# Moving ScalarE's Square pass over the mask from layer 0's slots to layer 1's

## The reference, cut to what matters

```python
x = layernorm(x + L0(x, adj))   # softmax over rows of leaky_relu(s1 + s2), masked by adj == 0
x = layernorm(x + L1(x, adj))   # masked by adj > 0, softmax over columns, then elu
x = layernorm(x + L2(x, adj))   # masked by adj > 0, softmax over rows, with a bias, then elu
x = layernorm(x + L3(x, adj))   # relation layer: one mask (adj == r) for each r of 1 to 4
```

## Time and profile before

| what | value |
|---|---|
| time of the kernel, median of 3 runs | 443.77 us |
| lowest and highest of the runs | 443.39 and 444.32 us |
| span of the profiled execution, first to last instruction | 440.8 us |
| the profiled execution's own time | not listed apart; the runs' times stand some 3 us above its span |
| busy, share of the span: PE, PEld, DVE, ACT, POOL | 83%, 74%, 84%, 72%, 67% |
| Square passes (L703) | 16, from 29.3 to 121.3 us, 1999 ns each |
| mean granted clock of TensorE | 0.952 |

### The profile page before, as it was taken

One profiled execution on the slowest core, in us unless ns is written; L12 is line 12 of the kernel. 1 busy time (PEld: TensorE's weight loads), 2 busy tenths in 40 slices (PEclk: granted clock), 3 DMA queues, 4 the chain that ended last, 5 costly groups with the idle time before them and its releaser, 6 DMA issues. The chain is left out here.

```text
span 440.8 us, 9222 instructions
## 1 busy us (share of the span) xinstructions
PE 366.6 (83%) x2770; PEld 326.6 (74%) x2777; DVE 368.5 (84%) x1406; ACT 316.0 (72%) x814; POOL 294.1 (67%) x430
## 2 busy tenths in 40 slices
PE   2689999999977776976787799899999789898860
PEld 1689999999877776876787799889888674454540
DVE  0067999999999999999999988889898987887862
ACT  2378999999855865655755867778787667877853
POOL 3226889977656644545463676888788867788782
PEclk9999999999988989898898999999999999999995
DMA  6999664000000000000000000000000000012122
GB/s 159 220 248 250 142 127 78 0 2 1 3 1 2 0 1 1 1 1 2 1 1 1 1 1 2 0 2 2 0 1 4 0 1 1 25 72 74 67 77 75
DMA packets 8756, 18.19 MB, mean 41 GB/s; under 512 B 1280, under 2 KB 2560, under 8 KB 8704
## 3 DMA queue, kind: packets, MB, share of 16 engines
q0 software_dynamic: 2304, 8.39, 10.0%
q1 hardware_dynamic: 5280, 8.72, 5.6%
q10 hardware_dynamic: 1120, 0.46, 0.5%
HBM read 21.76 MB, written 4.19 MB: 59 GB/s over the span
## 5 line engine op out<-in xcount | busy, mean ns | idle before, releaser
L486 PE MATMUL o_ps<-h_scaled,PT 128*128 128x129 f32 (+1 forms) x1536 | 190.3, 285 | 2.5 <-DVE PT L911 1.2
L486 PEld LDWEIGHTS o_ps<-h_scaled,PT 128*128 128x128 f32 x1536 | 186.2, 202 | 3.5 <-issue 1.7
L690 ACT ACTIVATE X<-y,offset,rstd 128x128 f32<-128x128 f32 x256 | 105.0, 481 | 47.9 <-POOL offset L277 47.9
L911 DVE SCALAR_TENSOR_TENSOR PT<-rows_ps,factors,MT 128x512 f32<-128x512 f32 x128 | 88.8, 737 | 0.6 <-PE rows_ps L473 0.2
L434 PE MATMUL h_ps<-wx,xT 128*128 128x130 f32 x384 | 58.8, 301 | 24.8 <-DVE smax L866 24.1
L434 PEld LDWEIGHTS h_ps<-wx,xT 128*128 128x128 f32 x384 | 52.5, 208 | 31.7 <-issue 31.5
L268 POOL TENSOR_TENSOR rstd<-var_eps,neg_half 128x4 f32<-128x4 f32 x64 | 68.9, 1077 | 5.0
L983 DVE BATCH_NORM_STATS2 stats<-y 128x6 f32<-128x128 f32 x256 | 56.0, 281 | 6.7 <-DVE y L963 0.5
L283 POOL TENSOR_TENSOR elu_exp<-elu_exp,X 128x512 f32<-128x512 f32 x32 | 40.8, 1274 | 15.0 <-ACT elu_exp L684 14.7
L258 POOL TENSOR_TENSOR h_scaled<-hx,factors 128x516 f32<-128x516 f32 x32 | 33.7, 1052 | 19.9 <-ACT factors L650 10.2
L906 DVE SCALAR_TENSOR_TENSOR PT<-MT,empty_col,edge 128x512 f32<-128x512 bf16 x64 | 44.3, 744 | 0.0
(11 more groups left out here) (104 smaller groups left out, 596.0 us busy)
## 6 DMA issues: line engine op xcount, KB each, us to landing
MT<-adj_by_j POOLq DMA_DIRECT2D x16, 512.0 KB, 8.8
X<-x SPq DMA_DIRECT2D x16, 256.0 KB, 6.5
out<-X SPq DMA_DIRECT2D x16, 256.0 KB, 2.0
w_rel<-w SPq DMA_DIRECT2D x1, 256.0 KB, 5.1
w_back<-w_by_output ACTq DMA_DIRECT2D x1, 192.0 KB, 3.3
wx<-w_by_input ACTq DMA_DIRECT2D x1, 192.0 KB, 5.5
bias<-b ACTq DMA_DIRECT2D x1, 64.0 KB, 4.6
bias<-b SPq DMA_DIRECT2D x1, 64.0 KB, 5.8
```

The costliest lines, as they stand in the source:

```text
L486: last = pe.matmul(o_ps[it.b][:, ic, first:1 + D], PT[:, it.b, jc, ic * P:(ic + 1) * P], h_scaled[:, it.b, jc, first:1 + D], start=(jc == ...
L690: last = act.activation(X[:, g, c, :], y[:, b, c, :], ACT.Identity, bias=offset[:, b, c:c + 1], scale=rstd[:, b, c:c + 1])
L911: dve.scalar_tensor_tensor(out=PT[:, it.b, c, :], in0=rows_ps[:], scalar=factors[:, it.b, 1, c:c + 1], in1=m, op0=ALU.max, op1=ALU.mult, * ...
```

## The change

The pass is called for `at(0)` at the end of ACT's `attention_slot`. The condition on the layer is the only thing that changes:

```diff
@@ -742,7 +742,7 @@
                 if n == -1:
                     act.wait_ge(sem("b2_ps"), 1)
                     act.copy(b2_a[:, :], o_ps[1][:, 0, 0:2]).then_inc(sem("b2_a"), 1)
-                if at(0) and at(0).l == 0:
+                if at(0) and at(0).l == 1:
                     flag(at(0))
 
             def relation_slot(at, n):
```

## The result

The changed kernel takes 465.65 us (median of 4 runs, 464.71 to 467.43), the kernel before, measured beside it, 443.58 (442.67 to 444.32). The ratio is 1.0502, with a 95% interval of 1.046 to 1.0544: slower by 22 us, near the forecast of 466.5 us and inside its range. The profiled execution is the run of 464.71 us; its span is 462.7, 21.9 us longer than before. The ratios in this document leave out two slow executions, one of 916.30 us in the first experiment and one of 452.32 us in the third, and no run shows what happened in them.

The account below looks back on a forecast made before the run. Bound: PE at 5.94 us a slot in layer 0, DVE at 8.28 in layer 1, where the change makes the ACT-POOL ring bind; -0.7 + 1.99 + 20.4 + 1.0 = +22.7 on span 440.8, plus 3.0: 466.5 us, range 456 to 472.

Parts of the forecast that it names:

- Layer 0, a gain of 0.7: Layer 0 loses 16 Squares; 13 slots go from 6.00 to 5.94 us each, gaining 0.7 us.
- The floor: Layer 0: PE still needs 5.94 us a slot without ACT's load.
- The upper bound of 5.1: Layer 0: the most to gain, 5.1 us, if only DVE's busy time of 5.61 us a slot were the limit.
- Slots 16 and 17, hidden: First two slots of layer 1: ACT's 4.03 us wait for PE's rows covers the passes, cost 0.
- Slot 18, +1.99: Layer 1, slot 18: the Square is exposed on ACT, so slot 19's take_rows starts 1.99 us later.
- The collision: Layer 1: late neg_mean and offset on POOL fall under DVE's line 906 and end only at its next 0.67 us step.
- Slots 19 to 30 at 9.88 us, +20.4: Layer 1: the closed ACT and POOL chain bounds 12 slots at 9.88 us, plus 2.15 for bias copies; 20.4 us lost.
- Slot 31, +1.0: Last slot of layer 1: 0 to 1.99 us of the pass shows, taken as 1.0.
- The rest gives nothing back: Everything else costs 0, and layer 2 and what follows pass ACT's lateness through whole.
- Rival A: Layer 1: POOL is not delayed by line 906, slots of 9.10 us, total +13.3, 457.1 us; chance 0.17.
- Rival B: Layer 1: POOL's rstd falls under line 906 too, 8.0 us more, 474.5 us; chance 0.13.
- Rival C: Layer 1: the pass hides within DVE's 8.28 us slot, 443.1 us, or 438.7 at the lower end; chance 0.07.

Follow-up runs that it names:

- the first experiment: The changed kernel with the same layer 1 passes moved ahead of the normalization in ACT's queue: 444.48 us, ratio 1.0008.
- the third: The kernel before, with POOL finding rstd and offset of the item before ahead of elu_low: 449.11 us, ratio 1.0102.

## Why the prediction was right, point by point

**Layer 0, a gain of 0.7.** Slots 0 to 13 took 77.66 us against 77.95, a gain of 0.29. The floor was right: most slots took 5.95 us. But two of 6.10 and 6.15 us (32.23 to 38.33, 62.19 to 68.34) came up though layer 0 has no pass any more, so the assumption that every slot would be at the floor failed here. In the experiment without a pass it held, with a gain of 0.72. Either gain is below what a run can tell. The upper bound of 5.1 is excluded by the experiment without a pass.

**Slots 16 and 17, hidden.** Right. ACT still waits for PE's rows before slot 18's take_rows; the cover was 4.03 us and has shrunk to 2.17, by nearly the price of a pass:

```profile
140.65 0.60 ACT L663 ACTIVATE q_rows<-rows_ps 128x512 f32<-128x512 f32 x1 [2.17 <-PE rows_ps L473]
```

**Slot 18, +1.99.** Too small. The slot took 10.04 us (140.65 to 150.69) in place of 7.51, 2.53 more. The term took the pass as all of it. The timeline shows the rest:

```profile
145.55 0.74 DVE L906 SCALAR_TENSOR_TENSOR PT<-MT,empty_col,edge 128x512 f32<-128x512 bf16 x1
145.56 0.79 POOL L273 TENSOR_TENSOR neg_mean<-mean_var,minus_one 128x4 f32<-128x4 f32 x1
...
147.06 1.65 ACT L690 ACTIVATE X<-y,offset,rstd 128x128 f32<-128x128 f32 x4 [1.57 <-POOL offset L277]
```

neg_mean began 0.01 us behind line 906 and took 0.79; in the kernel before it had begun 0.11 ahead (147.41 against 147.52) and took 0.20. elu_exp to normalization grew from 4.17 to 4.72 us. The collision that the prediction used from slot 19 on was there one slot earlier.

**Slots 19 to 30 at 9.88 us, +20.4.** Right: 9.90 us, but for the slot with the bias copies and slot 30 (9.44), and +20.22. In slot 24, counted from take_rows, edges stand at 1.09 (forecast 1.12), var_eps at 3.60 (3.61), the normalization at 6.27 (6.24). The bias copies added 2.18 us to slot 26, forecast 2.15. The step that this hung on, POOL's instructions ending at DVE's next step, is confirmed by the experiment that takes one of them away: 0.67 us a slot. neg_mean took 0.67 us; the prediction's signs said 0.4 to 0.5, while its own sum had 0.65.

The Trainium skill, in "SBUF — State Buffer", section "SBUF: two separate sides", describes a port that VectorE and GpSimd share as an exclusive lock: whichever starts first has it for its whole instruction, and the other waits. The trace agrees for neg_mean and offset, which began under an instruction of line 906 (205.07 and 205.89, under those of 204.95 and 205.62) and ended behind it. It does not agree for rstd, which began at 204.08, ahead of line 906 at 204.28: both ran side by side at their usual 1.02 and 0.73 us, where by the rule line 906 would have waited. The subsection on the bandwidth-pool intuition gives about 115 ns from the end of VectorE's work to the release of the other, for a DMA issued by GpSimd beside a copy of VectorE. The trace has that order of size: neg_mean and offset end 0.12 to 0.14 us behind the start of the next instruction of line 906, which is 0.05 to 0.07 behind the recorded end of the one that held them up.

**Slot 31, +1.0.** 1.13. The forecast had taken the middle between 0 and 1.99, so that it came so near is luck.

**The rest gives nothing back.** Right, to 0.13 us.

**Rival A** (9.10 a slot, no collision) fell with slot 24; with neg_mean out of the way the slot comes near to it, at 9.23. **Rival B** (rstd under line 906 too) missed by little: rstd began at 204.08, line 906 at 204.28, so by the prediction's sum 0.20 us separated 466 from 474 us. No run shows such slots; in slot 17 of the changed kernel, outside the ring, rstd began under line 906 (139.50 against 139.28) and took 1.41 us in place of 1.02. **Rival C** (hidden, since ACT is only 59% busy) fell, and the first experiment says why so strongly: with the same busy time of ACT, the kernel takes 444.48 or 465.65 us by the place of the pass in ACT's queue.

**The sum**, 22.7 against 21.9 of span, is closer than its terms, and that is luck: slot 18 was 0.5 too small, the stretch before it promised 0.5 too much (0.21 had been gained by slot 18's take_rows), and the launch, which no term held, gave 1.64 us that have nothing to do with the change. The 3.0 us assumed between span and median came to 2.95 (462.7 and 465.65); 2.0 of them belong to the profiled execution itself, which took 464.71 us. That a measurement of this kernel can tell 0.2% was too fine: the ratios above have intervals of 0.3 to 0.7% to either side.

## What to carry to other kernels

An engine's idle time is room only at the place in its program order where it idles: follow one slot from engine to engine until the chain closes, and compare the length of that ring with the fullest engine's slot before putting anything into it. When a ring is lengthened, look also at what its late legs now coincide with, since here that came to 0.8 us a slot beside the pass's 2.0. If a pass has to go into such a slot, put it just ahead of the wait that closes the ring, as the first experiment did.

## What the runs showed of the hardware that was not expected

POOL can hold up DVE, not only DVE POOL. node_terms is a small tensor_scalar of DVE (128x4, with a scalar per partition from SBUF); under POOL's elu_low (128x512 with two inputs in SBUF) it took 0.62 us instead of 0.22 and ended with it, in both kernels with the new order on POOL. 0.40 us in each of 12 slots is 4.8 us, against the 5 that these kernels lost.

The other direction the prediction had read from one slot, and the runs bear it out: behind a train of DVE instructions neg_mean and offset advance one at each boundary. Together they cost two steps of 0.67 us (1.35 from 205.07 to 206.42), though each alone needs 0.20, and with one of them gone a slot is one step shorter. rstd, which begins ahead of the train, keeps its 1.02 us.
